# Issuing the second half of the stack transfers at unit 12 of the first chunk instead of unit 26

## What is computed

```
h = tokenise(x, W)                    # (8, 1024, 64)
h = concatenate([h, txt], axis=1)     # (8, 1056, 64)
h = h + attention(layernorm(h))       # 4 heads of 16, softmax over 1056 keys, projection
h = h + experts(layernorm(h))         # 8 experts of width 128, exact gelu, the best 2 weighted
```

## Time and profile before

| | us |
|---|---|
| median of 3 runs | 995.42 |
| lowest and highest | 988.59, 1004.88 |
| profiled execution, its own time | 989.01 |
| profiled execution, span | 987.2 |
| TensorE busy in it | 877.0 |
| VectorE, ScalarE, GpSimd busy | 566.0, 484.4, 139.0 |

### The profile page before, as it was taken

The page is one execution under the profiler, slowest core; times in us unless marked ns, Lnnn a source line. Parts: engine busy times, 40 slices in busy tenths (PEclk is TensorE's granted clock), DMA queues, the critical chain, the costliest instruction groups (busy, mean ns, idle before and its releaser), DMA issues. The chain is left out here.

```text
span 987.2 us, 16297 instructions
## 1 busy us (share of the span) xinstructions
PE 877.0 (89%) x5964; PEld 354.9 (36%) x5964; DVE 566.0 (57%) x1212; ACT 484.4 (49%) x1165; POOL 139.0 (14%) x148
## 2 busy tenths in 40 slices
PE   5665899998999989999999999998866999898996
PEld 5240322432332342342243243332413445354443
DVE  4035665686784577775567778887131554636331
ACT  0020354564664555664445566665433545555552
POOL 0010100011010011010001101010001343434453
PEclk9965599997999999999979999998757899999998
DMA  8329441037532008724002206100007465382731
GB/s 151 59 46 161 77 54 34 1 47 119 99 64 60 2 3 127 134 38 87 1 2 46 34 3 85 38 14 2 1 16 177 88 144 107 88 174 62 154 74 23
DMA packets 56970, 66.53 MB, mean 67 GB/s; under 512 B 24501, under 2 KB 42561, under 8 KB 56897
## 3 DMA queue, kind: packets, MB, share of 16 engines
q1 hardware_dynamic: 56897, 65.56, 36.2%
HBM read 38.82 MB, written 2.57 MB: 42 GB/s over the span
## 5 line engine op out<-in xcount | busy, mean ns | idle before, releaser
L934 DVE TENSOR_REDUCE max_parts<-bank 128x1 f32<-128x512 f32 x512 | 331.2, 684 | 137.2 <-PE bank L1124 134.9
L856 ACT ACTIVATE probs<-bank 128x384 f32<-128x384 f32 (+1 forms) x768 | 311.8, 465 | 195.1 <-PE bank L1087 194.0
L1087 PE MATMUL bank<-q_stack,k_stack 99*128 99x384 bf16 (+1 forms) x768 | 231.1, 330 | 4.2 <-ACT probs L856 3.7
L1124 PE MATMUL bank<-k_stack,q_stack 96*128 96x512 bf16 x512 | 205.7, 405 | 16.8 <-DMA k_stack<-part 12.9
L1065 PE MATMUL bank<-probs,v_tiles 128*32 128x384 f32 (+1 forms) x1536 | 163.7, 501 | 2.4 <-ACT heads_out L841 2.3
L1087 PEld LDWEIGHTS bank<-q_stack,k_stack 99*128 99x128 bf16 x768 | 72.9, 100 | 205.8 <-ACT probs L856 150.7
L1335 ACT ACTIVATE hid<-bank,biases 128x352 f32<-128x352 f32 x192 | 96.0, 552 | 86.0 <-PE bank L1379 86.0
L1354 DVE SCALAR_TENSOR_TENSOR prod<-bank,biases,cwb 128x352 f32<-128x352 f32 x96 | 55.5, 581 | 118.9 <-PE bank L1367 101.9
L1379 PE MATMUL bank<-x,w 128*128 128x352 bf16 (+1 forms) x576 | 105.3, 320 | 6.3 <-DMA x<-part 6.3
L1367 PE MATMUL bank<-hid,w_sb 128*64 128x352 f32 x384 | 78.5, 488 | 8.7 <-DVE prod L1354 5.1
L815 POOL TENSOR_TENSOR part<-qk_rest,part 128x352 bf16<-128x352 f32 x24 | 20.4, 852 | 396.9 <-DVE part L982 396.9
(11 more groups left out here) (151 smaller groups left out, 647.9 us busy)
## 6 DMA issues: line engine op xcount, KB each, us to landing
cwb<-gates_by_expert SPq DMA_DIRECT2D x16, 1056.0 KB, 12.3
x<-in_x SPq DMA_DIRECT2D x64, 256.0 KB, 8.3
q_stack<-part SPq DMA_DIRECT2D x48, 132.0 KB, 4.5
k_stack<-part SPq DMA_DIRECT2D x48, 132.0 KB, 5.1
x<-part SPq DMA_DIRECT2D x32, 132.0 KB, 2.4
h_res<-h_new SPq DMA_DIRECT2D x4, 528.0 KB, 2.9
recip<-recip_rows SPq DMA_DIRECT2D x32, 66.0 KB, 2.6
h_all<-h_res SPq DMA_DIRECT2D x4, 528.0 KB, 6.2
```

What stands on the lines that cost most here:

```text
L856: nc.scalar.activation(probs[:, group % 3, h, 0:n], src, ACT.Exp, scale=SCALE).then_inc(exp_done, 1)
L934: nc.vector.tensor_reduce(max_parts[:, c, H * j + h, i % 2:i % 2 + 1], src[:, :], AX.X, ALU.max)\
L1087: last = nc.tensor.matmul(bank[:, 0:n], ks[par][0:ROWS + 3, h, P * kt:P * kt + P], qs[par][0:ROWS + 3, h, QC[qc]], start=True, stop=True)
L1124: last = nc.tensor.matmul(bank[:, :], queries(h, j), ks[par][0:ROWS, h, HALF * (i % 2):HALF * (i % 2) + HALF], start=True, stop=True)
```

## The change

One number of the table of units differs. The function `side_steps` puts `("stack", i)` at unit `AT_STACK[i]`, in slot 0 four units later.

```diff
@@ -54,7 +54,7 @@
 AT_RECIP = 8
 AT_NORMALISE = [24, 26, 28]
 AT_FINISH = [27, 30, 33]
-AT_STACK = [3, 26]
+AT_STACK = [3, 12]
 AT_EMBED = [list(range(34, 49, 2)), list(range(50, 65, 2))]
 AT_VARY = [74, 75, 76]
 AT_ROOT = [77, 78, 79, 80]
```

## The result

The changed kernel took 1014.11 us (median of 4 runs, 1011.76 to 1021.0), the kernel before 992.37 us beside it (4 runs). The ratio is 1.0244 with a 95% interval of 1.0165 to 1.0322: slower, by about 24 us by this ratio and 22 us between the medians.

The account below looks back on a forecast made before the run. TensorE, busy 89% of the 987.2 us span, was taken as the bound. Stalls +24.6, gaps gone -6.5, new falls +17.7, old falls gone -5.9 gave +29.9 us: 1019 on 989.0, 1025 on 995.4; forecast 1022, range 1000 to 1040.

Parts of the forecast that it names:

- The removed waits: Slots 1, 3, 5: L865's waits for k_stack go, with TensorE's idle (6.5 us) and old low-clock stretches (5.9 us).
- gaps: TensorE's idle before the second projection matmul in slots 1, 3, 5 goes: 2.46, 2.09 and 1.99 us, 6.5 in all.
- falls: Half-clock stretches of TensorE after two of those three idle times go, 4.4 + 1.5 = 5.9 us.
- The new wait: Unit 33 (L1083), slots 1 to 6, waits for the shift behind twelve stacks: 4.1 us each, 24.6 in all.
- the later bound: The shift lands 16.2 us after T0, the first group's first issue, as in the prologue; stall 4.9 us, slots 1 and 4.
- The clock: After each new stall, slots 1 to 6, TensorE's clock is half for 6.7 us, costing 2.9 us; six cost 17.7.
- Slot 0: No finishing sample, so the second group drains before the shift; unit 33 waits 0.24 us as before, effect zero.
- The sum: Whole kernel: +24.6 stalls, -6.5 gaps gone, +17.7 new falls, -5.9 old falls gone, +29.9 us.
- Not held back: Rival, 12%: the shift at unit 33 lands by T0+11.6, stall at most 2 us in all, kernel 10 us faster.
- No more falls: Rival, 20%: stalls at unit 33 come, but TensorE's clock falls no more often than now; +18 us, 1007 to 1013.
- Does nothing: Rival, 2%: SyncE does not follow units, so issuing the second group at unit 12 might be no earlier.
- TensorE might make up for the stalls: Sign of being wrong: in units after the stall TensorE had been waiting for ScalarE and VectorE; no size given.

Follow-up runs that it names:

- e5: In slots 1 to 6 only two of the second group's six stack transfers go ahead of the shift, four follow; ratio 0.9962 to the kernel before, median 986.35 us.
- e6: The reordered kernel: the changed kernel with the first stack group ahead of the wait for the reciprocals; ratio 0.9863 to the kernel before, median 981.06 us.
- e9: The reordered kernel, with GpSimd's normalising products waiting for VectorE's split of the second chunk's maxima; ratio 0.9804 to the kernel before, median 972.16 us.
- e3: The changed kernel, with the second chunk's shift issued by GpSimd with its own semaphore instead of SyncE; ratio 1.0322 to the kernel before.

## Why the prediction was right

**The removed waits.** Right in kind and size. The two terms, gaps (6.5 us) and falls (5.9 us) of the odd slots' second chunks, were put at 12.4 us. With both gone, as in e5, e6 and e9, these chunks take 23.8 us three times, against 84.1 us in all before: 12.7 us.

**The new wait.** Right in place and mechanism. The landing in the prologue gave the size: 15.2 to 16.2 us after T0 was forecast, 16.2 to 17.0 was measured (230.58 - 213.65 = 16.9 in slot 1), so the middle that I took was too early and the later bound was nearer. Six times 4.1 became 27.7 us for 24.6, and the first chunks as wholes grew by 29.4. The pixel loads behind the shift, put at nothing, may have their share: the landing is latest in slots 1 and 3, which issue them (16.9 and 17.0, the other four 16.2 to 16.4), and so it is in e3 (medians of 8.7 and 9.2 against 7.9 to 8.4). No run takes them away. The rule of the Trainium skill (DMA: Bandwidth & Descriptors, section "Why a DMA increments its semaphore by 16 and not by 1") that put the shift on three of 16 engines was read as an earlier landing; by that reading the six would have been 21.6, on the wrong side. "What is issued later on SyncE's queue waits" was right but too narrow: e3 shows that it waits from GpSimd's queue too.

**The clock.** A fall behind each of the six gaps was forecast, 6.7 us long at 2.9 us, and came, six times, 6.6 to 6.8 us long. The price was less: second chunks grew by 2.3, 2.1 and 2.8 us in the even slots, and in the odd ones they took 25.9, 25.7 and 26.3 where 23.8 is the time without a fall. That is 13.7 us (7.2 and 6.5) for the 17.7 of the sum. The step that was off is the length: the forecast charged the whole low stretch, but it begins inside the gap, where TensorE has nothing to do. The six rows of low clock in the section on the result hold 31.6 us of busy TensorE in 39.9 us of low stretch, and 13.7 by 31.6 is 0.43 per us, as the 0.44 of the forecast had it.

**Slot 0.** Put at nothing; its unit 33 waits 1.21 us instead of 0.24. The loads and stacks ahead of the shift were not drained, as I had it: the transfer engines are at a share of 1.00 to 1.21 from 130 to 135 us, where the kernel before has at most 0.09.

**The sum.** In the terms of the forecast: 29.4 (first chunks) + 13.7 - 12.7 = +30.4 us in slots 1 to 6, where 29.9 was forecast. That the two agree so closely is luck: the stalls were put too low by 4.8 us and their clock too high by 4.0. The kernel as a whole lost 22.8 us between the profiled executions. What lies between is the profiled execution of the kernel before, which held a low stretch of 13.5 us in slot 4 that stood behind another wait (5.6 us), and a time from slot 7 on that was 4.5 us longer. I had listed that stretch, and not asked whether the next execution would have it. The median beside the new runs, 992.4, was also 3 us lower than the 995.4 that stood before me.

**The rivals.** "Not held back" fell with the waits at L1083. "No more falls" fell at six low stretches. "Does nothing" fell with SyncE's timeline. That TensorE might make up for the stalls did not show: the third chunks are as long as before or longer by up to 0.6 us, but for slot 4's, which is shorter for the reason given.

## What to carry to other kernels

Before a bulk transfer is issued earlier, ask which small, late transfer it will now stand in front of, and whether its reader has as much slack as the backlog takes to drain; another issuing queue did not help here. A list that is ordered by "units" but waits on something else (here a reciprocal) has its real times in the trace, and the free time in it is ahead of that wait, not behind: moving the first group there made the same early second group a gain of 1.4% instead of a loss of 2.4%. And a single profiled execution can hold a low stretch that the next one lacks, here worth 5.6 us, so compare stretch by stretch before a difference of spans is put down to a change. A wait in front of TensorE is paid twice when the clock falls with it, so count both.

## What was unexpected in the hardware

A transfer of 3 KB issued by GpSimd landed 1.6 to 1.9 us after its issue on idle transfer engines and 7.6 to 10.1 us after it when ten to twelve stack transfers of 132 KB had been issued from SyncE in the 7 to 8 us before.

VectorE's product of 128x12 elements with both operands in SBUF took 0.17 us alone and, in the reordered kernel, eight times 0.58 to 0.83 us while GpSimd ran a product of 128x352 from SBUF; the cast between the two, one operand, kept its 0.17 us. The same is in the kernel before in slots 2 and 5, where L959 took 0.81 and 0.72 us, unnoticed. The Trainium skill, SBUF — State Buffer, section "Who interferes with whom", says that VectorE instructions with two SBUF inputs and GpSimd's reads exclude each other on a shared port; the rows agree, and e9, which keeps them apart, has 0.17 to 0.18 us for all 48.
